# The opening batch's row gathers, issued in two groups of eight with a full wait between the groups

## The reference

```python
rp   = concatenate([region_tbl[region_idx], poi_tbl[poi_idx]], -1)         # 8 + 4 wide, per sample and step
nv   = concatenate([rp @ W_rp + b_rp, coords @ W_co + b_co], -1)
conv = elu(conv1d(nv, conv_w) + conv_b)                                    # 3 taps: 10 steps become 8
emb  = tanh(concatenate([car_tbl[car_idx], week_tbl[week_idx], time_tbl[time_idx]], -1))
x    = concatenate([conv, broadcast(emb)], -1)
h    = lstm(x, Wih0, Whh0, ...)
h    = lstm(h, Wih1, Whh1, ...)
y    = ((h[:, -1] @ W1 + b1) @ W2 + b2) @ W3 + b3
```

## Time and profile before

| | us |
|---|---|
| median of 3 runs | 1096.57 |
| profiled execution, its own time | 1095.74 |
| span of the profiled execution (first to last instruction) | 1093.9 |
| PE busy | 1061.3 (97% of the span) |
| DVE, ACT, POOL busy | 744.0, 516.4, 322.9 |
| POOL: first gather of the opening starts | 6.54 |
| POOL: last of the 24 gathers ahead of `copy_emb` starts | 36.27 |
| POOL: `copy_emb` starts | 54.97 |
| PE: `turn_steps` of steps 0 to 3 starts | 50.29 |

### The profile page before, as it was taken

The page is one execution under the profiler, slowest core; times in us unless marked ns, Lnnn a source line. Parts: engine busy times, 40 slices in busy tenths (PEclk is TensorE's granted clock), DMA queues, the critical chain, the costliest instruction groups (busy, mean ns, idle before and its releaser), DMA issues.

```text
span 1093.9 us, 14380 instructions
## 1 busy us (share of the span) xinstructions
PE 1061.3 (97%) x4905; PEld 508.4 (46%) x4905; DVE 744.0 (68%) x1162; ACT 516.4 (47%) x757; POOL 322.9 (30%) x340
## 2 busy tenths in 40 slices
PE   6599999999999999999999999999999999999998
PEld 5444444444445444444445444444444544444445
DVE  4578986666867865657777776667676776666554
ACT  1466454434554544444554634445455544444433
POOL 7263056533440045552440025552441000000000
PEclk9799999999999999999999999999999999999999
DMA  9310010000011010000010110000010110000001
GB/s 265 63 18 16 10 23 3 2 2 1 12 21 39 1 33 3 2 2 1 2 31 1 39 32 3 3 2 2 3 31 1 39 29 1 1 0 1 0 1 39
DMA packets 32082, 21.26 MB, mean 19 GB/s; under 512 B 19629, under 2 KB 25865, under 8 KB 32019
## 3 DMA queue, kind: packets, MB, share of 16 engines
q1 hardware_dynamic: 21223, 19.25, 6.1%
q0 software_dynamic: 9984, 1.12, 2.6%
q10 hardware_dynamic: 812, 0.07, 0.1%
HBM read 9.92 MB, written 4.19 MB: 13 GB/s over the span
## 4 chain that ended last, share of the span: by engine, by line
PE 89%; DVE 5%; issue 3%; ACT 2%; DVEq 0%; ACTq 0%; POOL 0%; POOLq 0%
PE acc L1504 49%; PE acc L1495 27%; PE acc L1486 5%; PE aux L1696 2%; PE acc L1322 2%; PE acc L1529 1%; PE acc L1538 1%; DVE h_full L1176 1%; DVE gates L1129 1%; PE aux L1410 1%; DVE h_part L1177 1%; ACT gates L802 1%; PE aux L1449 1%; PE aux L1443 0%; ACT tanh_c L807 0%
## 5 line engine op out<-in xcount | busy, mean ns | idle before, releaser
L1504 PE MATMUL acc<-h_part,wh 128*128 128x512 f16 (+1 forms) x2640 | 644.3, 380 | 0.0
L1504 PEld LDWEIGHTS acc<-h_part,wh 128*128 128x128 f16 x2640 | 240.2, 98 | 314.2 <-issue 54.6
L1495 PE MATMUL acc<-h_part,wh 128*128 128x512 f16 (+1 forms) x1440 | 346.8, 379 | 0.0
L802 ACT ACTIVATE gates<-acc,gate_bias,unscale 128x512 f32<-128x512 f32 x246 | 189.3, 777 | 300.7 <-PE acc L1504 260.8
L802 ACT ACTIVATE gates<-gates,gate_bias,unscale 128x512 f32<-128x512 f32 x242 | 189.0, 811 | 142.9 <-DVE gates L1129 135.3
L1495 PEld LDWEIGHTS acc<-h_part,wh 128*128 128x128 f16 x1440 | 139.8, 98 | 171.5 <-issue 6.2
L623 POOL DMA_INDIRECT feat<-in_L_rec_region_tbl,region_idx x160 | 162.8, 1017 | 166.1 <-PE acc L1504 129.4
L1129 DVE TENSOR_TENSOR gates<-acc,emb_gates 128x512 f32<-128x512 f32 x242 | 160.6, 686 | 45.5 <-PE acc L1504 31.1
L623 POOL DMA_INDIRECT feat<-in_L_rec_poi_tbl,poi_idx x120 | 119.8, 998 | 109.6 <-PE acc L1504 90.1
L1486 PE MATMUL acc<-x_in,wx 96*128 96x512 f32 (+1 forms) x248 | 137.2, 559 | 5.0 <-DVE gates L1129 2.6
L1176 DVE TENSOR_TENSOR h_full<-gates,tanh_c 128x512 f32<-128x512 f32 x120 | 82.8, 690 | 75.3 <-ACT tanh_c L807 74.5
(11 more groups left out here) (179 smaller groups left out, 414.2 us busy)
## 6 DMA issues: line engine op xcount, KB each, us to landing
out<-y SPq DMA_DIRECT2D x16, 256.0 KB, 2.1
x_in<-conv_hi SPq DMA_DIRECT2D x56, 64.0 KB
feat<-in_L_rec_region_tbl,region_idx POOLq DMA_INDIRECT x160
w<-in_L_rec_W SPq DMA_DIRECT2D x4, 512.0 KB, 5.1
w_nat<-in_L_rec_Whh SPq DMA_DIRECT2D x2, 1024.0 KB
w<-in_L_rec_W SPq DMA_DIRECT2D x1, 2048.0 KB
feat<-in_L_rec_poi_tbl,poi_idx POOLq DMA_INDIRECT x120
x_in<-conv_lo SPq DMA_DIRECT2D x28, 64.0 KB
```

The lines of the kernel that those rows point to most:

```text
L802: nc.scalar.activation(gates[layer][:, j, g, :], source, ACT.Tanh if g == GATE_G else ACT.Sigmoid, bias=gate_bias[:, layer, m:m + 1], scal ...
L1495: mm = nc.tensor.matmul(bank, wh[:, 1, a, c, rows], h_part[0][:, s.write_slot, b, c, :], start=(c == 0 and a == b == HI), stop=(s.first an ...
L1504: mm = nc.tensor.matmul(bank, wh[:, own_w, a, c, rows], h_part[layer][:, s.read_slot, b, c, :], start=False, stop=(c == HK - 1 and a == LO))
```

## The change

Step 1 no longer stands beside step 2 in flight: ahead of step 2 POOL waits for both semaphores, so steps 0 and 1 (eight gathers) have landed before steps 2 and 3 (eight gathers) are issued, and step 3 has no wait of its own. Likewise the eight embedding gathers are issued in one go, once steps 2 and 3 have both landed. The number of gathers, their order, their targets and their semaphores stay as they are, and nothing else changes.

```diff
                     pool.wait_ge(idx_ready, 1)
                     for t in range(PAIR_WIN):
-                        if t >= 2:
-                            pool.wait_ge(rows_first_in[t % 2], GR * DMA)
+                        if t == PAIR_WIN // 2:
+                            pool.wait_ge(rows_first_in[0], GR * DMA)
+                            pool.wait_ge(rows_first_in[1], GR * DMA)
                         gather_steps(t, t + 1, False, rows_first_in[t % 2])
                     pool.wait_ge(small_put, 1)
-                    for g in range(0, GR, 2):
-                        pool.wait_ge(rows_first_in[g // 2], 2 * GR * DMA)
-                        gather_emb(g, g + 2)
+                    for half in range(2):
+                        pool.wait_ge(rows_first_in[half], 2 * GR * DMA)
+                    gather_emb(0, GR)
                     copy_emb()
```

## The result

The changed kernel takes 1082.75 us (1082.26 to 1083.97, four runs) against 1096.52 for the kernel before beside it (1096.06 to 1096.92, four runs). The ratio is 0.9877, 95% interval 0.9864 to 0.9890: 13.8 us, 1.23% faster. The forecast was 1096.6 and the range began at 1094.4, so the time lies outside, on the side that had 0.13. The profiled execution took 1083.97, with a span of 1082.2 us, 11.7 less than before.

A forecast was written before the change was run, and what follows sets the result against it. PE, busy for 97% of the 1093.9 us span, was taken as the bound, idle mostly in the opening. Terms summed to 0: 1095.74 + 0 = 1095.7, plus 0.83 for the median, forecast 1096.6, range 1094.4 to 1103.0.

The forecast's parts named there:

- the side that had 0.13: The outcome that the changed kernel is faster by over 0.2%, given a chance of 0.13.
- The steps on POOL: POOL's opening list: step 2 loses 2.1 us, the eight embedding gathers start 2.7 to 6.4 us later, taken as 6.
- The sum is 0 on the path: Whole kernel: 6 us of later gathers fall where 9 us of cover exist, so the time changes by 0.
- the hold: Opening, about 16 to 40 us: some of PE's results are seen late, cause not in the profile.
- Rival A: `poi_rows` and the product at 40.19: PE's restart moves with the embedding gathers, 6 us slower, 1102.6; chance 0.19.
- Rival B: PE in `poi_rows`: gathers off the engines from 28.7 to 33.5 us remove two pauses, 3.8 us faster, 1092.8; chance 0.13.
- The cover: POOL's 17.75 us wait for DVE's week rows before the copy at 54.97 hides the later gathers, 9.0 us left.
- rival C: POOL's wait doesn't suffice to hide the later embedding rows; 1 us late gives 1097.6; chance 0.02.
- The rule: Issue DMA early, wait late: the two new waits would cost POOL 2.0 us each, 4 us in all.

The follow-up runs named there:

- the fills of POOL: Changed kernel with four POOL memsets (some 2.4 us) behind every eighth gather in place of each of the two landing waits: 1085.22 us, ratio 0.9902.
- the kernel with the later loads: Kernel before with SP's weight loads from Wih1 on held until gather steps 0 to 3 have landed: 1097.08 us, ratio 1.0006 (nine runs).
- the second wait alone: Kernel before with only the joint wait ahead of all eight embedding gathers, steps 2 and 3 waiting as before: 1092.54 us.
- two fills after fours: Changed kernel with two POOL memsets (1.12 us) behind every fourth gather in place of the landing waits: 1080.42 us, ratio 0.9859.
- the short pause after fours: Changed kernel with one POOL memset (0.54 us) behind every fourth gather in place of the landing waits: 1091.72 us, ratio 0.9962.
- the first wait alone: Kernel before with only the new wait ahead of step 2, embedding gathers waiting as before in two fours: 1089.31 us.

## Why the prediction was wrong

**The steps on POOL were nearly right.** Gather 9 was forecast at 19.0 after 2.4 us and stands at 19.65 after 2.82, 0.17 of it because the whole list began that much later. Gather 13 has its 0.30 us. The first embedding gather stands at 34.48, 0.6 beyond the upper bound of 33.9, and the last at 43.23, beyond 42.7: the last gather of step 3 started 0.60 later than forecast (28.40), landed 5.29 us after its start in place of 5.5, and from there to the issue 0.79 passed in place of 0.6. The Trainium skill's fixed cost of about 2.0 us ("DMA: Bandwidth & Descriptors", "Anatomy of one DMA") fits neither pause: 2.82 and 5.13 us.

**The step that failed is "The sum is 0 on the path".** It rests on the hold not being touched. I had seen the hold, named it as the one place where this change could touch the time, and then priced it at nothing. It was worth 18.6 us at the product and 13.8 in the medians; of the terms on POOL the largest error is 0.9, the delay of the embedding gathers (6.94 in place of 6).

**The argument that misled** was that from 18.6 to 21.4 us no gather is on the engines while PE isn't released, used against both rivals. It looked for the cause among the packets. In that stretch POOL went on issuing, every 1.25 us from 16.93 on the earlier trace rows, and that is what counts: the fills of POOL show a release without a landing and with packets moving, and the kernel with the later loads shows a hold with the engines at 6.0%.

**Rival A** (the hold lasts as long as the gathers do) was right that the end of the hold follows the gathers, and tied it to the wrong event. It follows the last issue: 37.2 (36.27 + 0.94) and 40.9 in the kernel before, 36.4 and 40.5 without waits, 26.5 and 29.5 with the second wait alone. Moving the embedding gathers later by 7 us didn't make it longer, because the pauses had cut it in pieces. ACT of the kernel before:

```profile
22.70 0.37 ACT L736 COPY w_t<-acc 128x257 f32<-128x257 f32 x1 [8.15 <-issue]
...
40.90 0.37 ACT L736 COPY w_t<-acc 128x257 f32<-128x257 f32 x1 [16.23 <-remote]
```

The row at 22.70 also shows that single results get through in the middle of a run.

**Rival B** (a pause frees PE) had the direction, with "how much is in flight" for what is now POOL's issuing, and a price of 3.8 us. It counted only two of the pauses within `poi_rows` and not the 9.02 us ahead of it nor the wait behind it, which belong to the same hold: 18.6 us from 21.55 to 40.19 were at stake. Priced with all of the late results, the case would have read down to 1078.0 (1096.6 - 18.6), and the measured time lies inside it.

**The cover was no cover.** The 17.75 us that POOL waits for the week rows were there because DVE was late, and DVE because of PE. The week rows came from 54.40 to 40.49, by 13.9 us, and `copy_emb` now runs at 44.25 right behind the last gather. So rival C has come true in a small part: `turn_emb` waits 1.68 us for POOL's L653, and PE 1.33 us at 60.68 for steps 4 and 5, whose gathers start behind `copy_emb` (at 46.44, not "where they did", at 55.88). The forecast did say that week rows that move with PE would prove it wrong; the 9 us of cover ought to have been made to depend on that.

**Where 18.6 us became 12.** 3.5 went back ahead of L1348 (18.6 to 15.1), nearly all of it by the second, short hold: from the product to L1348 are 9.95 us here and 6.71 with two fills after fours; 1.3 more by `turn_steps`, most of it since the 16 transposes took 3.62 us and not 1.92, at half clock; 1.7 by `turn_emb` waiting for POOL. The first cell starts 13.1 us earlier (50.70, before 63.77), since its wait of 1.29 us for `x_in` is gone; the wait for steps 4 and 5 takes that back, and the second cell starts 12.0 us earlier (65.71, before 77.75). The span is 11.7 less. The medians differ by 13.8, the two profiled executions by 11.8: the changed kernel's was the slowest of its four, and that of the kernel before (1095.74) below all four of its runs.

**The rule** of the Trainium skill ("DMA: Bandwidth & Descriptors", "Rules for kernel authors"), to issue early and to wait late, speaks against the change. Here the two early waits made the kernel 13.8 us faster. That isn't because waiting pays: where each step waits for the one ahead, nothing is seen late and `turn_steps` still stands idle for 7.53 us. What pays is the pause in the issuing. Not issuing for 1.1 us after every fourth gather, with no wait for a landing, is worth 16.2 us (1096.62 less 1080.42), where there is a hold.

What stays open: by which path POOL's issuing keeps PE's results from being seen and PE's own matmuls from starting, and why the kernel before has the hold in some groups of runs (1096 to 1097) and not in others (1078.5 to 1078.9), on one and the same chip. Where it has none, the changed kernel itself was not measured, so whether it gains or loses there isn't known.

## What to carry to other kernels

When engines stand idle beside a long run of indirect gathers and the profile names no releaser for it, or shows a consumer starting many microseconds behind a producer that is recorded as done, put short pauses between the issues (here 1.1 us after four, or 0.54 us after two) before looking for contention in the DMA queues. A wait of another engine counts as cover only when its own releaser doesn't move with the thing that is in question. And an unexplained gap on the path has to be priced whole, as a rival of its own.

## What the runs showed of the hardware

- While POOL issues indirect gathers one behind the other (0.94 us each with 0.30 between them), results of TensorE reach ACT and DVE late, by up to 17.8 us of idle time at one instruction. The last late result comes 3.0 to 4.2 us behind the last issue where 16 or 24 gathers ran with at most 1.6 us of pause among them (3.0 with the second wait alone, 4.2 with the later loads), and 1.7 to 2.0 us behind it where the list was in eights or shorter runs (1.7 at the second eight of the changed kernel and with the fills after eights, 1.9 with the short pause after fours, 2.0 with the first wait alone).
- In the same stretches TensorE's own matmuls start 1.4 to 2.1 us apart where nothing is waited for between them (L1399 in the kernel before, L1330 with the short pause after fours).
- A pause in POOL's issuing without a wait for a landing, 17 to 18% of the time behind every second or fourth gather, keeps nearly all of it away (the latest result about 1.2 us late); 9% behind every fourth, 13% behind every sixth and 18% behind every eighth don't.
- It doesn't need any other DMA traffic: 6.0% of the engines' time, all of it the gathers', was in use from 18.5 to 27.5 us, when ACT stood idle for 12.10 us before a product at 26.49.
- The same program takes 1096 to 1097 us in some groups of runs and 1078.5 in others, 1.7% apart, with a spread of at most 0.5% inside a group.
